# Layer norm by per-token statistics and one activation per token and image; reciprocals read from PSUM

## The chip, the cores and the metric

The kernel runs on one core of a Trainium2 chip. The metric is the device time of one execution in microseconds (us). All data stay in the chip's memory before and after; nothing is computed on the host.

## The reference

The input is x, 16 images of 64 channels by 56x56 pixels, float32. Two layers follow each other.

```
x = x + conv(group_norm(x))                        # grouped correlations, two depthwise convolutions
t = tokens of x: 3136 per image, 64 channels
t = t + attention(layer_norm(t))                   # linear attention, 16 heads of 64, features elu + 1
t = t + experts(layer_norm(t))                     # 32 experts, routing by softmax over tokens
layer_norm(v) = (v - mean(v)) / sqrt(var(v) + 1e-5)      # over the 64 channels of one token
attention: q, k = elu(.) + 1, weighted by cos and sin of the position
           out = (q . sum k v) / (q . sum k + 1e-5)      # the division is by token and head
```

Only the two layer norms and the division of the attention are touched by the change.

## The kernel before

Images are worked on in 8 pairs, the two images side by side, so that a tile of 128 partitions holds 64 channels of both. Seven pairs run in a hardware loop on every engine, and in that loop the convolution of the next pair is computed beside the attention of this one; the eighth pair is a copy of the body without a next pair. A setup stage stands ahead and a final stage (expert matrices, additions, stores) behind. Every engine runs a list of its own in program order and waits on semaphores for the others, so the order written in the functions named pair_of_images is the order of the work.

A pair has these stages.

- **Key stage**, 50 tiles (25 of 128 tokens for each image). TensorE projects a tile (k_project), ScalarE takes the exponential, VectorE makes the feature (k_features), GpSimd weights the tokens by cos and sin, and TensorE multiplies (k_products).
- **Query stage**, 56 slots: 14 steps (7 blocks of 448 pixels for each image) by 4 quarters of the 16 heads. In slot j TensorE projects quarter j (q_project), ScalarE takes its exponential into EQ, and VectorE makes the feature of quarter j-1 (q_features). Later slots deal with quarters that are further along: denominators (den_parts, den_guard, den_reciprocal), reciprocals stored to memory and loaded again, spread over the partitions, into RB by SyncE's queue, the multiplication of a feature by its reciprocal (q_scale, line 1118), the output product (q_output), its weighting (out_parts), the fold and the residual (out_residual). The lags in slots are constants.
- **Drain**, slots 56 to 68, in which the last quarters are finished and the front of the next pair's convolution is computed.
- **Correlations and back**: TensorE's correlations for the next pair, the routing of this pair, the next pair's convolution, and the first layer norm of its first two groups of tokens.

Tokens are normalised in NG = 4 groups of 7, 7, 7 and 4 tiles of 128 tokens, both images at once: 14 or 8 rows of 64 channels on each partition. The first norm (LN1) has groups 0 and 1 in the back stage and groups 2 and 3 in the key stage; the second norm (LN2) has groups 0 and 1 in the query stage and groups 2 and 3 in the drain and after it. norm_part is four parts on VectorE: sums, means and subtraction, squares, sums of squares. deviations, on GpSimd, turns a group's variances into 1/sqrt; norm_scale, on VectorE, multiplies. In LN1 ScalarE's high_part and VectorE's low_part then split the result in two float16 halves for TensorE.

Beside this, in tiles 20 to 49 and slots 3 to 47, 75 taps of the next pair's depthwise convolution are computed: ScalarE multiplies a shifted window by a weight (tap_product, line 723) and GpSimd adds it up (tap_sum, line 591). VectorE has other taps (depthwise, line 936), which lie in the key stage and after the query stage.

PSUM is cut in areas A, B and C of two banks and D and E of one. In the query stage A and B alternate between quarters, E holds denominators and their sums, and outputs alternate between D and C, where C holds the folds too. Each use of an area waits until the one before it was emptied.

## Time and profile before

| | |
|---|---|
| time, median of 3 runs | 3789.2 us (3786.9 to 3798.8) |
| the profiled execution | 3803.7 us, its span 3801.8 us |
| TensorE matmuls busy | 3253.6 us, 86% of the span |
| VectorE busy | 2995.8 us, 79% |
| ScalarE busy | 1746.2 us, 46% |
| GpSimd busy | 1561.9 us, 41% |
| mean granted TensorE clock | 0.942 |

A share of busy time is a mean over stages with different limits. Stages repeat pair by pair, so that one pair of the seven in the loop can be read for all, and the eighth pair shows the same stages without the convolution's work beside them.

### The profile page before, as it was taken

How to read it: one execution, taken by the hardware profiler on the slowest of the kernel's cores; microseconds unless marked ns; L12 is line 12 of the kernel's file. 1: busy time of each engine (PE TensorE's matmuls, PEld its weight loads, DVE VectorE, ACT ScalarE, POOL GpSimd, SP SyncE). 2: the span in 40 equal slices, each digit the busy share in tenths (PEclk: the TensorE clock that was granted, in tenths of full speed). 3: DMA queues.
4: the chain of work that ended last, by engine and by line, in shares of the span. 5: the costliest groups of instructions: out<-in, count | busy, mean ns of one | idle time of the engine just before them, and what ended most of it. 6: DMA issues, size and time to landing. Idle time of an engine off the chain costs nothing.

```text
span 3801.8 us, 50528 instructions
## 1 busy us (share of the span) xinstructions
PE 3253.6 (86%) x16628; PEld 1480.5 (39%) x16628; DVE 2995.8 (79%) x3283; ACT 1746.2 (46%) x1881; POOL 1561.9 (41%) x1078
## 2 busy tenths in 40 slices
PE   4698888988898888988889888898889888898965
PEld 2343334433443335433344334433354333543333
DVE  6887987889687987879878796788877798756843
ACT  1166524754357533665347543465335653343320
POOL 1067611864038631676218650287414762210000
PEclk8899999999999998999999999999999999999977
DMA  2002540044200551025400453005520155204566
GB/s 51 18 1 60 129 105 27 1 109 117 67 27 17 132 128 44 1 60 124 111 27 1 100 117 77 27 1 129 123 51 19 30 129 118 49 1 95 132 155 232
DMA packets 69379, 279.57 MB, mean 74 GB/s; under 512 B 30845, under 2 KB 35485, under 8 KB 64221
## 3 DMA queue, kind: packets, MB, share of 16 engines
q1 hardware_dynamic: 69085, 275.89, 29.8%
q8 instruction: 155, 2.54, 0.3%
q14 instruction: 139, 1.14, 0.1%
HBM read 242.78 MB, written 33.05 MB: 73 GB/s over the span
## 4 chain that ended last, share of the span: by engine, by line
PE 49%; DVE 25%; issue 10%; DMA 8%; ACT 4%; SPq 2%; POOL 1%; DVEq 0%; POOLq 0%; ACTq 0%
PE ps_C L1474 9%; DVE region L1118 5%; PE ps_A L1459 5%; PE ps_B L1459 5%; DMA RB<-r_keep 5%; PE ps_D L1474 4%; DVE region L1110 4%; PE ps_E L1474 4%; PE ps_D L1541 4%; PE ps_C L1541 3%; PE ps_E L1520 3%; DVE arena L936 3%; PE ps_D L1327 3%; PE ps_B L1503 2%; DMA r_keep<-RR 2%
## 5 line engine op out<-in xcount | busy, mean ns | idle before, releaser
L591 POOL TENSOR_TENSOR arena<-arena,UHL 128x896 f32<-128x896 f32 x525 | 1136.9, 2169 | 473.2 <-ACT UHL L723 473.2
L1118 DVE TENSOR_TENSOR region<-region,RB 128x896 f32<-128x896 f32 x448 | 647.0, 1445 | 97.1 <-DMA RB<-r_keep 96.9
L723 ACT ACTIVATE UHL<-arena,W8C 128x896 f32<-128x896 f32 x525 | 542.0, 1032 | 0.0
L569 POOL TENSOR_SCALAR ST<-ST 128x14 f32<-128x14 f32 x64 | 23.7, 371 | 1125.6 <-DVE ST L991 1124.3
L759 ACT ACTIVATE EQ<-ps_B,NEG 128x896 f32<-128x896 f32 x224 | 225.7, 1007 | 545.4 <-PE ps_B L1503 545.4
L1541 PE MATMUL ps_C<-region,small 128*128 128x448 f32 x896 | 409.7, 582 | 24.5 <-DVE region L1118 24.5
L1541 PE MATMUL ps_D<-region,small 128*128 128x448 f32 x896 | 405.7, 577 | 28.0 <-DVE region L1118 28.0
L601 POOL TENSOR_TENSOR UA<-region,CS 128x128 f32<-128x128 f32 (+1 forms) x400 | 229.7, 576 | 419.8 <-PE ps_C L1474 370.7
L1474 PE MATMUL ps_C<-region,UA 128*128 128x512 f32 (+1 forms) x800 | 378.3, 595 | 1.4 <-ACT region L657 1.3
L936 DVE SCALAR_TENSOR_TENSOR arena<-arena,W8C 128x448 f32<-128x448 f32 (+1 forms) x243 | 365.1, 1523 | 0.0
L1520 PE MATMUL ps_E<-region,small 128*32 128x448 f32 x1792 | 231.0, 589 | 155.5 <-DVE region L1110 154.7
L759 ACT ACTIVATE EQ<-ps_A,NEG 128x896 f32<-128x896 f32 x224 | 225.5, 1006 | 267.9 <-PE ps_A L1503 267.9
L1086 DVE SCALAR_TENSOR_TENSOR region<-region,ps_A 128x1024 f32<-128x1024 f32 (+1 forms) x200 | 242.2, 1211 | 106.0 <-ACT region L741 104.2
L1086 DVE SCALAR_TENSOR_TENSOR region<-region,ps_B 128x1024 f32<-128x1024 f32 (+1 forms) x200 | 242.4, 1212 | 105.4 <-ACT region L741 103.6
L741 ACT ACTIVATE region<-ps_A,NEG 128x1024 f32<-128x1024 f32 (+1 forms) x200 | 222.7, 1114 | 199.4 <-PE ps_A L1459 199.4
L741 ACT ACTIVATE region<-ps_B,NEG 128x1024 f32<-128x1024 f32 (+1 forms) x200 | 222.9, 1115 | 168.9 <-PE ps_B L1459 168.8
L1110 DVE SCALAR_TENSOR_TENSOR region<-EQ,ps_B 128x896 f32<-128x896 f32 x224 | 237.4, 1060 | 45.5 <-ACT EQ L759 39.7
L1110 DVE SCALAR_TENSOR_TENSOR region<-EQ,ps_A 128x896 f32<-128x896 f32 x224 | 241.5, 1078 | 26.7 <-ACT EQ L759 23.0
L1541 PEld LDWEIGHTS ps_C<-region,small 128*128 128x128 f32 x896 | 166.3, 199 | 203.9 <-issue 135.1
L1541 PEld LDWEIGHTS ps_D<-region,small 128*128 128x128 f32 x896 | 161.4, 195 | 212.3 <-issue 153.1
L1474 PE MATMUL ps_D<-region,UA 128*128 128x512 f32 (+1 forms) x400 | 205.9, 596 | 0.0
L1474 PE MATMUL ps_E<-region,UA 128*128 128x512 f32 (+1 forms) x400 | 204.2, 592 | 0.0
(296 smaller groups left out, 5063.9 us busy)
## 6 DMA issues: line engine op xcount, KB each, us to landing
RB<-r_keep SPq DMA_DIRECT2D x448, 448.0 KB, 5.8
arena<-x SPq DMA_DIRECT2D x8, 1568.0 KB, 7.2
t_keep<-Y SPq DMA_DIRECT2D x7, 1568.0 KB, 5.2
r_keep<-RR SPq DMA_DIRECT2D x448, 7.0 KB, 1.9
w_keep<-region SPq DMA_DIRECT2D x7, 784.0 KB, 5.9
CST<-t_keep SPq DMA_DIRECT2D x2, 1568.0 KB, 9.2
small<-t_keep SPq DMA_DIRECT2D x2, 1568.0 KB, 12.8
plane<-w_keep SPq DMA_DIRECT2D x4, 784.0 KB, 15.9
```

Of the source, the lines that this page charges most:

```text
L591: pool.tensor_tensor(out=X[:, cut], in0=X[:, cut], in1=PRODUCT[m % 3], op=ALU.add).then_inc(pool_taps.sem, 1)
L723: act.activation(PRODUCT[m % 3].rearrange("p (h w) -> p h w", w=W), g_window(2 * g * ROWS + 2 * (k // 5), 2 * (k % 5) - 4, 2 * ROWS), ACT. ...
L741: act.activation(E[0:r, k % 2], here.area(("kp", k))[0:r, :], ACT.Exp, bias=NEG1[0:r, 0:1]).then_inc(e_ready.sem, 1)
L759: act.activation(EQ[:, j % 2], here.area(key)[:, :] .rearrange("p (c n) -> p c n", c=2)[:, :, 0:PIX], ACT.Exp, bias=NEG1[:, 0:1]).then_inc ...
L936: dve.scalar_tensor_tensor(out=chunk, in0=window, scalar=w[:, k:k + 1], in1=chunk, op0=ALU.mult, op1=ALU.add).then_inc(taps_done.sem, 1)
L1086: dve.scalar_tensor_tensor(out=KT[0:r, k % 3], in0=E[0:r, k % 2], scalar=1.0, in1=here.area(key)[0:r, :], op0=ALU.min, op1=ALU.max)\
L1110: dve.scalar_tensor_tensor(out=Q[s % 3][:, 2 * cc:2 * cc + 2, :], in0=EQ[:, cc % 2], scalar=1.0, in1=here.area(key)[:, :].rearrange("p (c ...
L1118: dve.tensor_tensor(out=q, in0=q, op=ALU.mult, in1=RB[:, cc].rearrange("p (c n) -> p c n", c=2)).then_inc(scaled.sem, 1)
L1459: ins = pe.matmul(here.area(key)[0:r, cut], UTS[i][:, t * P:t * P + r], w[:, cut], start=m == 0, stop=m == 1)
L1474: ins = pe.matmul(dst, UA[0:r, k % 3].rearrange("p s c -> p (s c)"), KT[0:r, k % 3, n * 512:(n + 1) * 512], start=t == 0, stop=t == TILES - 1)
L1520: ins = pe.matmul(here.area(key)[j * STRIP:(j + 1) * STRIP, 0:PIX], KK[i][:, c, :], Q[s % 3][:, c, :], start=g == 0, stop=g == 1)
L1541: ins = pe.matmul(here.area(key)[:, 0:PIX], MW[i][:, c, :], Q[s % 3][:, c, :], start=c == 0, stop=c == NCHUNK - 1)
```

## The change

The layer norms get their statistics from bn_stats and bn_aggr on VectorE, one of each for every tile and image (14 or 8 of each in a group). GpSimd's deviations reads variance and mean from MVL and also makes minus mean times 1/sqrt. The subtraction and the multiplication become one Identity activation on ScalarE for every tile and image (apply_norm), in place, with scale and bias from ST. In the key stage, the query stage and the drain a group's activations are split over two tiles or slots. LN2's slots move, ALL_SLOTS grows by one, and low_part of groups 2 and 3 moves by one tile.

The spread reciprocals are copied by ScalarE from RB to PSUM area C (spread_out, at the lag that q_scale had), the steps from q_scale on come one slot later, and q_scale reads its second operand there. Outputs use D alone, and folds use E. SyncE loads the next half of RB when ScalarE has copied it, not when VectorE has used it. Stage by stage all other work stays where it was.

```diff
--- before.py
+++ after.py
@@ constants
-SPLIT_TILES = [None, 0, 9, 13]
+SPLIT_TILES = [None, 0, 10, 14]
...
-DEN_LAG, SUM_LAG, RECIP_LAG, RB_LAG, OUT_LAG, PARTS_LAG, FOLD_LAG = 4, 5, 5, 9, 10, 14, 19
-FOLD_SLOTS = {8 * n + FOLD_LAG: n for n in range(NPIX)}
+DEN_LAG, SUM_LAG, RECIP_LAG, COPY_LAG, RB_LAG, OUT_LAG, PARTS_LAG = 4, 5, 5, 9, 10, 11, 15
+FOLD_SLOTS = {8 * n + (22 if n < NPIX - 2 else 20): n for n in range(NPIX)}
...
-LN2_SLOTS = {28: 0, 44: 1, 60: 2, 68: 3}
-ALL_SLOTS = 69
+LN2_SLOTS = {31: 0, 47: 1, 61: 2, 69: 3}
+ALL_SLOTS = 70
@@ PSUM areas by use, in pair_uses
-                uses += [(("fold", FOLD_SLOTS[j]), "C")] if j in FOLD_SLOTS else []
+                uses += [(("fold", FOLD_SLOTS[j]), "E")] if j in FOLD_SLOTS else []
...
+                uses += [(("rb", *divmod(j - COPY_LAG, 4)), "C")] if 0 <= j - COPY_LAG < SLOTS else []
...
-                uses += [(("out", (j - OUT_LAG) // 4), "DC"[(j - OUT_LAG) // 4 % 2])] if slot_of_step(j, OUT_LAG) else []
+                uses += [(("out", (j - OUT_LAG) // 4), "D")] if slot_of_step(j, OUT_LAG) else []
@@ SyncE, before it loads half h of RB
-                            sp.wait_ge(*scaled.at(pair, 4 * (s - 1) + 2 * h + 2))
+                            sp.wait_ge(*here.filled(("rb", s - 1, 2 * h + 1)))
@@ GpSimd, deviations
+                st, mv = ST[:, g % 2], MVL[:, g % 2]
                 pool.wait_ge(*sums.at(pair, g + 1))
                 passed(pool)
-                pool.tensor_scalar(ST[:, g % 2, 2, :], ST[:, g % 2, 1, :], 1.0 / C, LN_EPS, ALU.mult, ALU.add)\
-                    .then_inc(variance.sem, 1)
-                pool.wait_ge(*turn)
-                pool.tensor_tensor(out=ST[:, g % 2, 3, :], in0=ST[:, g % 2, 2, :], op=ALU.pow,
-                                   in1=NEGH[:, 0:1].broadcast_to([P, 2 * GROUP])).then_inc(std.sem, 1)
+                pool.tensor_scalar(st[:, 2, :], mv[:, :, 1], LN_EPS, None, ALU.add)
+                pool.tensor_scalar(st[:, 1, :], mv[:, :, 0], -1.0, None, ALU.mult).then_inc(variance.sem, 1)
+                pool.wait_ge(*turn(1))
+                pool.tensor_tensor(out=st[:, 3, :], in0=st[:, 2, :], op=ALU.pow,
+                                   in1=NEGH[:, 0:1].broadcast_to([P, 2 * GROUP])).then_inc(variance.sem, 1)
+                pool.wait_ge(*turn(2))
+                pool.tensor_tensor(out=st[:, 0, :], in0=st[:, 1, :], in1=st[:, 3, :], op=ALU.mult)\
+                    .then_inc(std.sem, 1)
@@ ScalarE, new functions
+            def apply_norm(which, std, ready, pair, g, part=None):
+
+                t, m = GROUPS[g]
+                if part != 1:
+                    act.wait_ge(*std.at(pair, g + 1))
+                wide = C if which == 2 else C - 1
+                for n in range(m if part == 1 else 0, m if part == 0 else 2 * m):
+                    u = UN[which][:, 2 * t + n, 0:wide]
+                    ins = act.activation(u, u, ACT.Identity, bias=ST[:, g % 2, 0, n:n + 1],
+                                         scale=ST[:, g % 2, 3, n:n + 1])
+                if part != 0:
+                    ins.then_inc(ready.sem, 1)
...
+            def spread_out(here, s, cc):
+                key = ("rb", s, cc)
+                act.wait_ge(*spread_loaded[cc // 2].at(here.pair, s + 1))
+                act.wait_ge(*here.room(key))
+                passed(act)
+                act.activation(here.area(key)[:, :].rearrange("p (c n) -> p c n", c=2)[:, :, 0:PIX],
+                               RB[:, cc].rearrange("p (c n) -> p c n", c=2), ACT.Copy)\
+                    .then_inc(*here.fill(key))
@@ ScalarE, where they stand
                 for g in range(2):
+                    apply_norm(1, ln1_std, un1_ready, pair, g)
                     high_part(pair, g)
...
-                    if k in SPLIT_TILES[2:]:
-                        high_part(pair, SPLIT_TILES.index(k))
+                    for part in range(2):
+                        if k - part in SCALE_TILES:
+                            apply_norm(1, ln1_std, un1_ready, pair, SCALE_TILES.index(k - part), part)
+                    if k + 1 in SPLIT_TILES[2:]:
+                        high_part(pair, SPLIT_TILES.index(k + 1))
...
+                    if 0 <= j - COPY_LAG < SLOTS:
+                        spread_out(here, *divmod(j - COPY_LAG, 4))
                     if j in LN2_SLOTS:
                         tokens(here, 2, LN2_SLOTS[j])
+                    for part in range(2):
+                        if j - 7 - part in LN2_SLOTS:
+                            apply_norm(2, ln2_std, un2_ready, pair, LN2_SLOTS[j - 7 - part], part)
...
+                apply_norm(2, ln2_std, un2_ready, pair, NG - 1)
@@ VectorE, norm_part
-                    link(dve.tensor_reduce(out=st[:, 0], in_=u, axis=AX.X, op=ALU.add))
-                    link(dve.tensor_scalar(st[:, 3], st[:, 0], 1.0 / C, None, ALU.mult))
-                elif part == 1:
-                    link(dve.tensor_tensor(out=u, in0=u, in1=st[:, 3].unsqueeze(2).broadcast_to([P, 2 * m, C]),
-                                           op=ALU.subtract))
-                elif part == 2:
-                    link(dve.tensor_tensor(out=SQ[:, 0:2 * m, :], in0=u, in1=u, op=ALU.mult))
+                if part < 2:
+                    for n in range(part * m, (part + 1) * m):
+                        ins = dve.bn_stats(out=BSL[:, g % 2, n, :], in_=UN[which][:, 2 * t + n, :])
+                    if part == 1:
+                        link(ins)
+                        passed(dve)
+                        if which == 1:
+                            dve.memset(UN[1][:, 2 * t:2 * t + 2 * m, C - 1:C], 1.0)
                 else:
-                    dve.tensor_reduce(out=st[:, 1], in_=SQ[:, 0:2 * m, :], axis=AX.X, op=ALU.add)\
-                        .then_inc(sums.sem, 1)
+                    for n in range(2 * m):
+                        ins = dve.bn_aggr(out=MVL[:, g % 2, n, :], in_=BSL[:, g % 2, n:n + 1, :])
+                    ins.then_inc(sums.sem, 1)
...
-            def norm_scale(which, std, pair, g):
...
-                return dve.tensor_tensor(out=u, in0=u, op=ALU.mult,
-                                         in1=st[:, 3].unsqueeze(2).broadcast_to([P, 2 * m, C]))
-
-            def norm1_scale(pair, g):
@@ VectorE, q_scale
-                dve.wait_ge(*spread_loaded[cc // 2].at(here.pair, s + 1))
+                dve.wait_ge(*here.filled(key))
                 dve.tensor_tensor(out=q, in0=q, op=ALU.mult,
-                                  in1=RB[:, cc].rearrange("p (c n) -> p c n", c=2)).then_inc(scaled.sem, 1)
+                                  in1=here.area(key)[:, :].rearrange("p (c n) -> p c n", c=2)[:, :, 0:PIX])\
+                    .then_inc(*here.empty(key))
@@ TensorE, q_output
-                pe.wait_ge(*scaled.at(here.pair, 4 * s + cc + 1))
+                pe.wait_ge(*here.emptied(("rb", s, cc)))
```

The rest of the diff removes the semaphore `scaled` and the tile SQ, adds the tiles BSL and MVL with a memset, and fits the counts of semaphores and the calls of the functions above.

## Rows read from the trace of the kernel before

**Rows 1.** Stages of the fourth pair, and the last pair's query stage; duration, then PE, PEld, DVE, ACT, POOL busy.

```profile
1067.80:1202.00 134.20, 133.22 (x438) 57.78 (x437) 115.71 (x105) 90.38 (x92) 91.16 (x80) 0.99 0.03 12
...
1213.00:1404.70 191.70, 162.63 (x758) 62.73 (x756) 170.38 (x169) 99.33 (x103) 105.51 (x49) 0.96 0.52 118
1404.70:1436.50 31.80, 28.77 (x165) 11.43 (x163) 22.88 (x26) 8.83 (x17) 0.60 (x1) 1.00 0.53 117
1436.50:1512.00 75.50, 59.96 (x558) 39.28 (x558) 52.46 (x71) 25.59 (x30) 14.68 (x11) 0.90 0.13 38
...
3445.60:3620.80 175.20, 157.60 (x758) 62.45 (x756) 145.44 (x174) 57.80 (x58) 5.58 (x4) 0.98 0.58 130
```

**Rows 2.** Sum of the seven query stages of the loop, same columns, then their means.

```profile
sum 1346.40, PE 1140.69 PEld 440.28 DVE 1194.95 ACT 695.54 POOL 738.66; mean PE 162.96 PEld 62.90 DVE 170.71 ACT 99.36 POOL 105.52
```

**Rows 3.** Groups of instructions in the fourth pair's query stage: busy us, mean ns.

```profile
L1118 DVE TENSOR_TENSOR region<-region,RB 128x896 f32<-128x896 f32 x47 | 73.7, 1569 | 4.1 <-DMA RB<-r_keep 4.1
L723 ACT ACTIVATE UHL<-arena,W8C 128x896 f32<-128x896 f32 x45 | 46.5, 1033 | 0.0
...
L1110 DVE SCALAR_TENSOR_TENSOR region<-EQ,ps_B 128x896 f32<-128x896 f32 x27 | 28.6, 1059 | 4.5 <-ACT EQ L759 3.7 <-PE ps_C L1541 0.4 <-DVE SQ L989 0.4
L759 ACT ACTIVATE EQ<-ps_B,NEG 128x896 f32<-128x896 f32 x28 | 28.2, 1007 | 66.6 <-PE ps_B L1503 66.6
...
L1125 DVE TENSOR_TENSOR DS<-ps_E,CST 128x448 f32<-128x448 f32 x13 | 8.0, 617 | 4.4 <-PE ps_E L1520 4.3
...
L1003 DVE TENSOR_TENSOR un<-un,ST 128x896 f32<-128x896 f32 x2 | 3.7, 1842 | 0.0
...
L984 DVE TENSOR_SCALAR ST<-ST 128x14 f32<-128x14 f32 x2 | 3.1, 1540 | 0.1
```

**Rows 4.** The same in the last pair's query stage, where GpSimd adds no taps.

```profile
L1118 DVE TENSOR_TENSOR region<-region,RB 128x896 f32<-128x896 f32 x47 | 51.0, 1084 | 11.7 <-DMA RB<-r_keep 11.7
```

**Rows 5.** Timeline of the fourth pair's query stage: start us, duration us, instruction.

```profile
1212.95 1.01 ACT L759 ACTIVATE EQ<-ps_A,NEG 128x896 f32<-128x896 f32 x1 [5.90 <-PE ps_A L1503]
...
1213.86 1.00 ACT L759 ACTIVATE EQ<-ps_B,NEG 128x896 f32<-128x896 f32 x1
...
1304.77 2.09 POOL L591 TENSOR_TENSOR arena<-arena,UHL 128x896 f32<-128x896 f32 x1 [0.70 <-ACT UHL L723]
...
1305.85 1.96 DVE L1118 TENSOR_TENSOR region<-region,RB 128x896 f32<-128x896 f32 x1
```

**Rows 6.** Groups over the whole span, forms kept apart: small ones, and with a pointer operand or none.

```profile
L655 ACT ACTIVATE un<-ps_B 128x896 f32<-128x896 f32 x24 | 21.8, 910 | 19.7 <-PE ps_B L1378 19.7
...
L779 ACT ACTIVATE region<-ps_B,GBC 64x448 f32<-64x448 f32 x24 | 15.1, 630 | 11.7 <-PE ps_B L1616 11.4
...
L773 ACT ACTIVATE plane<-ps_A 128x448 f32<-128x448 f32 x8 | 4.5, 560 | 5.4 <-PE ps_A L1607 5.4
...
L683 ACT ACTIVATE region<-ps_B 64x64 f32<-64x64 f32 x7 | 1.4, 205 | 0.0
...
L1100 DVE COPY small<-ps_A 64x4 f32<-64x4 f32 x60 | 6.9, 156 | 0.2
...
L884 DVE BATCH_NORM_AGGREGATE MV<-BS 128x2 f32<-128x42 f32 x8 | 2.8, 345 | 1.2 <-DVE BS L880 0.5
```

**Rows 7.** Timeline of the back stage before the fifth pair's first key tile.

```profile
1490.92 1.09 DVE L983 TENSOR_REDUCE ST<-region 128x14 f32<-128x896 f32 x1
...
1495.50 1.08 DVE L983 TENSOR_REDUCE ST<-region 128x14 f32<-128x896 f32 x1
...
1500.08 1.08 DVE L1003 TENSOR_TENSOR region<-region,ST 128x896 f32<-128x896 f32 x1
...
1502.32 1.09 DVE L1015 TENSOR_TENSOR UHL<-region,UHL 128x896 f16<-128x896 f32 x1 [0.83 <-ACT UHL L663]
...
1505.72 0.55 PE L1391 MATMUL ps_E<-IDH,UHL 128*128 128x128 f16 x7 [1.42 <-DVE PT L1046]
...
1510.09 0.60 PE L1459 MATMUL ps_A<-WKH,plane 128*128 128x512 f16 x1 [3.82 <-issue]
```

More of the change, by code:

```diff
@@ L994, in norm_sums @@
             def norm_sums(here, which, sums, g):
-                for part in range(4):
+                for part in range(3):
                     norm_part(here, which, sums, g, part)
-            def norm_scale(which, std, pair, g):
-                t, m = GROUPS[g]
-                u = UN[which][:, 2 * t:2 * t + 2 * m, :]
-                st = ST[:, g % 2, :, 0:2 * m]
-                dve.wait_ge(*std.at(pair, g + 1))
-                return dve.tensor_tensor(out=u, in0=u, op=ALU.mult,
-                                         in1=st[:, 3].unsqueeze(2).broadcast_to([P, 2 * m, C]))
```

40 lines of the change are left out of this document (16 added, 24 removed).

## The prediction

> **What bounds the kernel now.** I read the busy shares first, then a table of stages, then the groups of the query stage, then its timeline. The shares (TensorE 86%, VectorE 79%) name no bound, since stages differ. In the table of stages [rows 1] the key stage is TensorE's: 133.2 us of 134.2 busy, so VectorE's savings there are worth nothing. The query stage is nobody's at first sight: 191.7 us with TensorE at 162.6 and VectorE at 170.4. The last pair does the same query work in 175.2 us, with TensorE at 157.6. What it lacks is GpSimd's taps (POOL 5.6 instead of 105.5) and ScalarE's products for them. VectorE has no taps in either, yet needs 25.0 us less (145.4). So GpSimd's work makes VectorE's slower, and that is the 16.5 us between the two stages. Seven such stages take 1346.4 us, 192.3 each [rows 2].
>
> The groups say where. q_scale takes 1569 ns in the loop's stage [rows 3] and 1084 ns in the last pair's [rows 4]. The timeline shows how: a tap starts on GpSimd at 1304.77 and lasts to 1306.86; q_scale, issued at 1305.85, has two inputs in SBUF and lasts 1.96 us, that is until about 0.95 us after the tap's end [rows 5]. It waits for the tap and only then runs. q_features, which has one input in PSUM, takes 1059 ns beside the same taps, and den_parts 617 ns for half the columns [rows 3]. An input in PSUM keeps an instruction out of this.
>
> **The change: reciprocals from PSUM.** q_scale gets that form, so I price it at 1.065 us. Its bounds are 1.059 (q_features) and 1.084 (its own uncontended time). 47 of them in a query stage save 47 x (1.569 - 1.065) = 23.7 us of VectorE. ScalarE gets 47 copies more. No row has it write to PSUM, so the copy lies between 0.91 us (a read of PSUM, no pointer operand) and 1.03 (tap product) [rows 3, 6]. Consecutive activations overlap: two exponentials of 1.01 us start 0.91 apart [rows 5]. In a slot with a product ScalarE then has about 0.91 + 0.93 + 0.88 = 2.7 us, at most 3.07 without overlap. TensorE's floor for a slot is 175.2 / 56 = 3.13 us. So ScalarE fits, with 0.1 to 0.4 us to spare in each of the 40 or so slots that have all three.
>
> The copies bring new waits. Area C is single, so a copy waits for the q_scale before it, and q_scale for its copy: 1.0 + 1.0 + two semaphores, 2.2 us, under a slot. The exponential behind a copy in ScalarE's order ends some 4.2 us after the slot's start on VectorE, and is due two slots after it, at 6.3: 2 us of slack. Outputs have only D now: q_output's first quarter waits for out_parts, which stands right behind q_features in VectorE's slot. Folds are in E, so the next denominators wait for out_residual, 2.9 us into VectorE's slot. But TensorE is the late one by then. From the second half of a step's denominators on it has two and a half outputs, three projections and the sums, some 8 us of its 12.5 in the step, before it comes to either wait. I price both at nothing. Uncovered, they cost about 1 us in each of 14 steps. For the loads of RB the buffer comes free about a slot's third later than before and is due as much later, so no change.
>
> **The change: layer norms.** On VectorE a full group's sums take 4.58 us now (1490.92 to 1495.50) and the scaling 1.08 [rows 7], and more beside GpSimd: in the query stage the 14-column step takes 1.54 us and the scaling 1.84 [rows 3]. So 5.7 to 7.6 us go for each group. They are replaced by 14 bn_stats and 14 bn_aggr. From 156 ns at 4 columns [rows 6] and 1.08 us at 896 [rows 7] a column costs 1.04 ns, so bn_stats of 64 columns takes 0.22 us and bn_aggr between 0.156 and 0.345 [rows 6]. With about 0.1 overlapped, a group is 14 x (0.12 + 0.15) = 3.8 us; bounds 2.4 (14 x 0.17) and 7.9 (no overlap, 0.345). I take 4.0. Two groups in the query stage give VectorE 7 us more; its load falls to 170.4 - 23.7 - 7 = 140 us, below the last pair's 145.4.
>
> On ScalarE a group is 14 activations with two pointer operands. A 64-column activation without pointers takes 205 ns; one pointer costs 0.07 (630 against 560 ns) to 0.10 (1007 against 910) [rows 3, 6]. So 0.205 + 0.17 = 0.375, started 0.28 to 0.3 apart: 4.0 us a group, bounds 14 x 0.1 = 1.4 and 14 x 0.4 = 5.6.
>
> The Trainium skill (ScalarE: Activation LUTs, What ACT_TABLE_LOAD costs) gives 186 ns + 0.833 ns per element, 93 ns for each pointer operand and 93 ns of overlap, which would be an estimated 0.33 us each and 4.6 us a group. By it the losses below would be a seventh higher.
>
> GpSimd has two small operations more in deviations, about 0.2 and 0.3 us.
>
> **Where the norm's new work lies.** Query stage: group 0 falls into two slots that also have products, 2 us of activations in each, against 2 us of slack and 0.4 regained per slot. I take 2 us lost. Group 1 comes after the products and is covered. Key stage: two tiles in a row get 2 us each on ScalarE beside exponential and high_part, 3.3 and 4.1 us against 2.68 for a tile; 0.8 us lost. Drain: half of group 2 now stands in front of the tokens of group 3, from which the correlations start; 1.0 us. Back: group 0's chain was sums, power, scaling, high_part, low_part at 1502.32, transposes at 1505.72, next key stage at 1510.09 [rows 7]. Now 4 us on ScalarE stand where 1.08 us on VectorE stood, less 0.6 from the sums, plus 0.5 on GpSimd; low_part comes 2.4 to 3 us later. But before, the transposes waited 1.4 us for the routing's copies behind a second scaling that is gone. So they come about 1.1 us later, and ScalarE, with group 1 behind them, makes the first exponential some 0.5 later still: 1.5 us.
>
> **The sum.** The query stage goes from 192.3 to 175.2, the last pair's floor, plus 2 for group 0 and 2 for the tighter coupling of three engines: 179.3, a gain of 13.0. Taken off are 0.8 + 1.0 + 1.5 = 3.3, which leaves 9.7 a pair, 68 us in seven. The last pair and the setup have no GpSimd taps to escape from and pay 6: their last groups lie open. Net -62 us. The profiled execution, 3803.7 us, would come to 3742; it stood 14.5 above the median, and from the median I get 3727.
>
> **Rivals.**
> - *The floor is reached and the norms hide.* The query stage comes to 175 or a little less, since TensorE still waits in the last pair, and the small activations cost half: 17 x 7 - 1 x 7 - 2 = 110 us, 3679. For it: VectorE's load falls under the last pair's. Against: ScalarE goes from 99 to 154 us of the stage. Chance 0.13.
> - *ScalarE's order becomes the bound of the query stage.* A slot then takes what exponential, product and copy need with their waits, 3.3 to 3.4 us where all three stand: 40 x 3.35 + 16 x 3.13 = 184, a gain of 8, and with 4 more for group 0 and 3.3 elsewhere it is next to nothing: -35 to +10, 3754 to 3799, middle 3780. For it: 3.07 us without overlap. Against: the overlap seen in consecutive exponentials. Chance 0.15.
> - *Slower: the small activations lie open.* A pair has 100 of them, 6 x 14 + 2 x 8. At 0.28 to 0.4 us that is 28 to 40 us of ScalarE, in front of exponentials in its order. If 20 us of it reach the path, 13.0 - 20 = -7, and 7 pairs with the 6 us of the ends make it 55 us slower: 3844. It decides from 13 us exposed on, against my 5.3 in all. For it: in the key stage TensorE has 1 us of slack. Chance 0.12.
>
> The Trainium skill (VectorE: DVE Perf Modes, The TRN2 errata) has a rule on that side: operations from SBUF on both engines pay a fixed time for each instruction, and tiles of 512 elements or more should be used. No row here has 64-column activations from SBUF with two pointers; if the rule holds for them, the time is that of this rival or between it and the forecast.
>
> **Chances and range.** The forecast, a query stage shorter by 9 to 16 us and a kernel shorter by 25 to 90, has 0.60. Measurements of this kernel can tell 0.3%, 11 us, from no change. Faster by more than that: 0.60 + 0.13 + a third of the second rival = 0.78. Within it: 0.09, from the second rival. Slower: 0.13, the third and the last of the second. The likeliest case alone would be 3700 to 3760. The range, 3675 to 3785, takes in the floor at the low end and most of the second rival at the high one, and leaves out the slower case.
>
> **What the profile after would show.** q_scale near 1.07 us in all stages, with or without GpSimd; the loop's query stage at 177 to 182 us, ScalarE at about 154 of them; the copy near 0.9 to 1.0 us; the small activations near 0.37 us and 0.28 apart; the key stage longer by about 1 us, and the first key tile 1 to 2 us later behind the sums of LN1. The prediction falls if exponentials come late in many slots, that is if VectorE's idle time behind them (3.7 us a stage for area B now [rows 3]) doubles, or if TensorE waits for VectorE at the first quarter of outputs or at denominators after a fold.

## The result, and the profile after

The changed kernel takes 3733.4 us (median of 4 runs, 3729.7 to 3743.7), the kernel before 3790.7 on the same chip (4 runs, 3786.9 to 3798.8). The ratio is 0.985, with a 95% interval of 0.9825 to 0.9876: 57 us less, where 62 were forecast.

The two profiled executions differ by more, 3803.7 against 3729.7 us. The one of before stood 14.5 us above its median of then, the one of after 3.7 below its own. Stage by stage below, 74 us are therefore shared out, and some 17 of them are the spread of single runs.

Shares and groups over the whole span of the kernel after, for [rows 3, 6]:

```profile
PE 3202.3 (86%) x16628; PEld 1465.8 (39%) x16628; DVE 2668.4 (72%) x4499; ACT 2375.5 (64%) x3129; POOL 1550.8 (42%) x1207
L1144 DVE TENSOR_TENSOR region<-region,ps_C 128x896 f32<-128x896 f32 x448 | 485.5, 1084 | 121.6 <-ACT ps_C L755 117.7
L755 ACT ACTIVATE ps_C<-RB 128x896 f32<-128x896 f32 x448 | 409.4, 914 | 167.7 <-DVE region L1144 99.2
```

q_scale is at 1084 ns over all stages and the copy at 914. VectorE fell from 79% to 72% of the span. Now the windows of one pair's key, query, drain and back stages and of the last pair's query stage, and the sum and mean of the seven query stages (columns as in [rows 1, 2]). The pair is the one that [rows 1] call the fourth. Counted from the first key exponential of the trace it is the third, and is called so from here on:

```profile
1056.00:1191.00 135.00, 132.67 (x433) 56.82 (x432) 111.65 (x137) 97.29 (x114) 92.22 (x84) 0.99 0.00 1
1201.90:1375.60 173.70, 153.96 (x754) 59.71 (x752) 139.55 (x212) 143.39 (x171) 100.38 (x53) 1.00 0.60 131
1375.60:1414.10 38.50, 32.09 (x169) 13.09 (x167) 24.36 (x52) 19.85 (x35) 3.49 (x3) 0.96 0.42 93
1414.10:1492.20 78.10, 59.78 (x567) 39.77 (x566) 41.85 (x122) 42.09 (x81) 14.08 (x17) 0.93 0.16 53
...
3374.80:3542.30 167.50, 154.84 (x754) 60.70 (x752) 140.43 (x217) 104.26 (x126) 6.68 (x8) 0.99 0.61 136
...
sum 1215.90, PE 1080.22 PEld 418.74 DVE 977.10 ACT 1003.78 POOL 702.73; mean PE 154.32 PEld 59.82 DVE 139.59 ACT 143.40 POOL 100.39
```

The query stage went from 192.3 us [rows 2] to 1215.9 / 7 = 173.7. VectorE's load in it fell from 170.7 to 139.6, ScalarE's rose to 143.4, and TensorE's fell too, from 163 to 154.3. Its matmuls are the same but for the four of one fold, some 1 us, which now lie in the drain (754 records for 758): the rest is the granted clock, 1.00 where it was 0.96. The last pair's query stage, 175.2 before, is 167.5. So what the prediction called a floor was none.

The stages of all kernels, from here on, as means over the seven loop pairs. Key is from the first to the last key exponential; 10.9 us follow in every kernel, then query, from its first to its last exponential; drain reaches to the last output product, back to the next pair's first key exponential. The slots of query and drain were shifted against each other by the change, so their sum is what compares. The last column is the time against that of before measured beside it on the same chip, with its 95% interval. The medians come from several chips, on which before took 3790.6 to 3795.7 us.

| kernel | key | query | drain | q. + d. | back | median us | ratio |
|---|---|---|---|---|---|---|---|
| before | 135.6 | 192.3 | 31.9 | 224.2 | 75.7 | 3790.7 | 1 |
| after | 136.2 | 173.7 | 37.6 | 211.3 | 78.1 | 3733.4 | 0.985 |
| reciprocals_only | 135.7 | 177.6 | 38.1 | 215.7 | 73.4 | 3715.8 | 0.9788 (0.9765 to 0.9811) |
| norms_only | 137.0 | 178.8 | 31.5 | 210.3 | 80.7 | 3742.6 | 0.9858 (0.9833 to 0.9883) |
| sbuf_read | 136.3 | 188.4 | 39.8 | 228.1 | 82.1 | 3879.3 | 1.0226 (1.0207 to 1.0246) |
| one_activation | 135.4 | 172.7 | 37.2 | 209.9 | 70.2 | 3646.4 | 0.9612 (0.9592 to 0.9631) |
| less_norm | 134.6 | 181.7 | 30.1 | 211.8 | 75.8 | 3707.3 | 0.9781 (0.9752 to 0.981) |
| half_output | 136.9 | 177.3 | 38.8 | 216.1 | 79.2 | 3772.7 | 0.9946 (0.9927 to 0.9965) |
| copy_twice | 136.9 | 195.3 | 43.2 | 238.5 | 77.9 | 3938.7 | 1.038 (1.0359 to 1.0402) |
| tokens_first | 136.6 | 172.2 | 35.0 | 207.2 | 77.7 | 3704.8 | 0.9766 (0.9746 to 0.9786) |
| vector_tokens | 135.4 | 172.0 | 35.0 | 207.0 | 73.3 | 3666.1 | 0.9678 (0.9657 to 0.9698) |
| vector_wide | 134.8 | 172.3 | 35.0 | 207.3 | 72.1 | 3644.6 | 0.9611 (0.9595 to 0.9627) |
| reciprocals_tokens | 135.2 | 175.3 | 35.2 | 210.5 | 74.1 | 3694.9 | 0.9752 (0.9731 to 0.9773) |
| vector_all | 134.6 | 173.4 | 35.7 | 209.1 | 71.2 | 3661.3 | 0.9647 (0.9627 to 0.9668) |

### The profile page after: what moved, and what is told of

Same layout as the page of the kernel before. It is cut to its first block, busy times and chain, and to the rows that moved or that the text cites. A ratio compares the mean times of both kernels' runs of the same rounds, so it can differ in the third digit from the quotient of the medians.

```text
span 3727.9 us, 54224 instructions
## 1 busy us (share of the span) xinstructions
PE 3202.3 (86%) x16628; PEld 1465.8 (39%) x16628; DVE 2668.4 (72%) x4499; ACT 2375.5 (64%) x3129; POOL 1550.8 (42%) x1207
## 4 chain that ended last, share of the span: by engine, by line
PE 44%; DVE 15%; ACT 15%; issue 11%; DMA 11%; SPq 3%; POOL 1%; ACTq 0%; DVEq 0%; POOLq 0%
PE ps_C L1496 8%; DMA RB<-r_keep 6%; PE ps_D L1563 5%; PE ps_A L1481 5%; PE ps_D L1496 5%; PE ps_E L1496 5%; PE ps_B L1481 4%; DMA r_keep<-RR 4%; ACT region L677 3%; PE ps_D L1349 3%; DVE arena L977 2%; PE ps_E L1542 2%; ACT ps_C L755 2%; ACT EQ L794 2%; DVE region L1144 2%
## 5 line engine op out<-in xcount | busy, mean ns | idle before, releaser
L600 POOL TENSOR_TENSOR arena<-arena,UHL 128x896 f32<-128x896 f32 x525 | 1092.5, 2085 | 425.5 <-ACT UHL L746 425.5
L1563 PE MATMUL ps_D<-region,small 128*128 128x448 f32 x1792 | 779.0, 560 | 71.6 <-DVE OS L1171 40.8
L1144 DVE TENSOR_TENSOR region<-region,ps_C 128x896 f32<-128x896 f32 x448 | 485.5, 1084 | 121.6 <-ACT ps_C L755 117.7
L755 ACT ACTIVATE ps_C<-RB 128x896 f32<-128x896 f32 x448 | 409.4, 914 | 167.7 <-DVE region L1144 99.2
L1563 PEld LDWEIGHTS ps_D<-region,small 128*128 128x128 f32 x1792 | 313.4, 190 | 427.7 <-issue 324.8
L572 POOL TENSOR_SCALAR ST<-MVL 128x14 f32<-128x14 f32 x64 | 26.7, 416 | 1055.8 <-DVE MVL L1032 1053.3
L773 ACT ACTIVATE region<-ps_B,NEG 128x1024 f32<-128x1024 f32 (+1 forms) x200 | 222.4, 1112 | 136.3 <-PE ps_B L1481 136.3
L1542 PE MATMUL ps_E<-region,small 128*32 128x448 f32 x1792 | 216.7, 555 | 63.6 <-DVE region L1135 61.8
L1135 DVE SCALAR_TENSOR_TENSOR region<-EQ,ps_A 128x896 f32<-128x896 f32 x224 | 241.4, 1078 | 37.2 <-ACT EQ L794 36.5
L1525 PE MATMUL ps_A<-plane,WQH 128*128 128x448 f16 x448 | 158.5, 354 | 56.1 <-DVE region L1135 22.4
L1496 PEld LDWEIGHTS ps_C<-region,UA 128*128 128x128 f32 (+1 forms) x800 | 153.1, 193 | 132.4 <-issue 106.2
```

The lines of the kernel that those rows point to most:

```text
L600: pool.tensor_tensor(out=X[:, cut], in0=X[:, cut], in1=PRODUCT[m % 3], op=ALU.add).then_inc(pool_taps.sem, 1)
L755: act.activation(here.area(key)[:, :].rearrange("p (c n) -> p c n", c=2)[:, :, 0:PIX], RB[:, cc].rearrange("p (c n) -> p c n", c=2), ACT.C ...
L773: act.activation(E[0:r, k % 2], here.area(("kp", k))[0:r, :], ACT.Exp, bias=NEG1[0:r, 0:1]).then_inc(e_ready.sem, 1)
L1135: dve.scalar_tensor_tensor(out=Q[s % 3][:, 2 * cc:2 * cc + 2, :], in0=EQ[:, cc % 2], scalar=1.0, in1=here.area(key)[:, :].rearrange("p (c ...
L1144: dve.tensor_tensor(out=q, in0=q, op=ALU.mult, in1=here.area(key)[:, :].rearrange("p (c n) -> p c n", c=2)[:, :, 0:PIX])\
L1496: ins = pe.matmul(dst, UA[0:r, k % 3].rearrange("p s c -> p (s c)"), KT[0:r, k % 3, n * 512:(n + 1) * 512], start=t == 0, stop=t == TILES - 1)
```

## The experiments

### Each half alone

reciprocals_only has the copies to PSUM with the layer norms of before; norms_only has the new layer norms with q_scale reading RB. Each is the one half of the diff above, with the lags and slots of its half; LN2's new slots went with the copies.

> The kernel before with the reciprocals' half of the change alone (copy to PSUM, lags, areas, LN2's slots); the layer norms stay on VectorE as before. My theory: the gain is q_scale's freedom from GpSimd, so q_scale is 1.08 us in all stages, query stage and drain together fall from 224 us to 212 to 215, key stage and back stage stay at 135.6 and 75.7, and the time is 3700 to 3725 us, a little under the changed kernel's 3733. Rival, the norms bring the gain: 3765 or more.

> The changed kernel without the reciprocals' half; q_scale reads RB in SBUF, with the old lags and areas. My theory: q_scale stays near 1.55 us in the loop's query stages, VectorE's lighter norms give some 2 us there, key and back stage lose 3 us together, and the time is 3780 to 3805 us, no gain. Rival, the norms bring the gain: 3760 or less.

Measured: 78 us less with the copies alone, and 51 less with the norms alone, where my theory gave the norms no gain. Together they bring 57: less than the copies alone. So the first expectation's theory held, but so did the second's rival, that the norms bring a gain. In norms_only q_scale still takes 1400 ns on average over all stages (1445 before) and 1512 in the third pair's query stage (1569), so most of its gain is not q_scale's. Query stages of the third pair, reciprocals_only and then norms_only:

```profile
1197.30:1375.10 177.80, 157.09 (x753) 60.26 (x752) 146.70 (x168) 136.70 (x150) 100.10 (x49) 0.98 0.56 129
```

```profile
1214.80:1393.20 178.40, 157.50 (x758) 61.90 (x756) 158.06 (x213) 108.25 (x131) 109.47 (x53) 0.97 0.55 126
```

The norms took 12.6 us off VectorE in the stage (170.7 to 158.1) and the stage lost 13.5; the copies took off 24.0 and the stage lost 14.7. From either one the other half takes only 4 to 5 us more: VectorE goes from 158.1 to 139.6 us and the stage from 178.8 to 173.7, about a quarter of the relief; after the copies it goes from 146.7 to 139.6 for 3.9 us, about half. So the norms' relief was worth its full size where it came first, the larger one of the copies some 60%, and each about half of that as the second.

With the drain, which the copies lengthen, the halves look different: query and drain are 13.9 us shorter with the norms alone, 8.5 with the copies alone, and 12.9 with both. On top of the norms the copies gain nothing there, as they stand in this change; what they add a pair is 2.6 us in the back stage (80.7 to 78.1) and 0.8 in the key stage, and the runs don't show why. (One query stage of norms_only, the first pair's, took 185.9 us; the other six have 177.6 in the mean.)

### A relief of VectorE and nothing else

less_norm is the kernel before; the layer norm over the outputs (LN2) leaves out the subtraction and the squares.

```diff
+                elif which == 2 and part < 3:
+                    return
```

> The kernel before without the subtraction and the squares of LN2 (parts 1 and 2; this leaves out part of the second norm). VectorE has 2.2 us less a group, 4.3 us in a query stage, and nothing else changes. Theory A, up to some 12 us the query stage follows VectorE's busy time one for one: query stage 192.3 - 4.5 = 188 us, last pair 175.2 - 4.3 = 171, and the time falls by 30 to 45 us. Theory B, the norms shortened the stage in another way (their moved slots, fewer waits of VectorE on itself): less than 2 us a stage, under 15 us in all.

Measured: 3707.3 us, 86 less, nearly twice the most that I expected. This is its third pair's query stage and the last pair's:

```profile
1191.60:1373.70 182.10, 158.72 (x758) 61.91 (x756) 163.36 (x165) 99.36 (x103) 108.73 (x49) 0.97 0.53 124
...
3352.00:3518.40 166.40, 154.03 (x758) 61.66 (x756) 140.78 (x171) 57.82 (x58) 5.58 (x4) 1.00 0.61 136
```

For 7.0 us less on VectorE the stages of the loop lost 10.6; the last pair's lost 8.8 (175.2 to 166.4) for 4.7 us less. ScalarE and GpSimd had nothing new. 4.6 of the 7.0 us are the parts left out; 2.1 are q_scale, which met fewer taps (1524 ns in the third pair's stage, 1569 before). TensorE's busy time fell as well, from 162.6 to 158.7 us for the same 758 matmuls. What the relief sets free is seen in the kernel before, in windows of 6 us around LN2's group in the third pair, and in instructions of VectorE there:

```profile
1308.00:1314.00 6.00, 2.56 (x8) 0.85 (x8) 5.60 (x5) 3.18 (x4) 2.93 (x2) 1.00 0.63 153
1314.00:1320.00 6.00, 5.31 (x24) 1.99 (x24) 5.77 (x6) 0.17 (x1) 3.24 (x3) 0.72 0.42 104
...
1326.00:1332.00 6.00, 3.23 (x16) 1.10 (x13) 6.00 (x5) 3.74 (x4) 3.68 (x3) 1.00 0.62 153
1332.00:1338.00 6.00, 6.00 (x26) 2.39 (x27) 5.26 (x6) 0.93 (x2) 1.33 (x1) 0.72 0.42 93
```

```profile
1302.55 1.54 DVE L984 TENSOR_SCALAR ST<-ST 128x14 f32<-128x14 f32 x1
...
1310.03 2.32 DVE L1118 TENSOR_TENSOR region<-region,RB 128x896 f32<-128x896 f32 x1
...
1328.31 2.60 DVE L1003 TENSOR_TENSOR un<-un,ST 128x896 f32<-128x896 f32 x1
```

VectorE is full there (5.6 and 6.0 of 6 us), with operations of the norm and q_scales stretched by the taps. TensorE has little to do (2.56 and 3.23 of 6 us), and in the next 6 us the granted clock is at 0.72, part of the time at its 1.2 GHz level, just when TensorE has the backlog to work off. The stall is paid twice. That less_norm, with nothing else changed, raised the clock of the last pair's stage from 0.98 to 1.00 and cut both stages by more than VectorE was relieved of is the evidence for this. The 48 us around this group, before and then after:

```profile
1290.00:1338.00 48.00, 38.83 (x174) 15.11 (x174) 45.25 (x42) 21.65 (x24) 26.18 (x13) 0.93 0.47 109
```

```profile
1291.00:1339.00 48.00, 42.40 (x203) 16.37 (x202) 38.58 (x71) 42.48 (x57) 32.39 (x18) 1.00 0.61 134
```

After the change, the clock is at 1.00 throughout, and 203 matmuls are done where 174 were.

### Is TensorE the floor now?

half_output is the kernel after with one of two matmuls of each q_output left out; half of the heads are missing from the outputs. copy_twice is the kernel after with one more activation of the copy's size ahead of each copy.

```diff
-                for c in (2 * cc, 2 * cc + 1):
+                for c in (2 * cc,):
```

```diff
+                act.activation(SPARE[:, :], RB[:, cc], ACT.Copy)
```

> The changed kernel with one of the two matmuls of each q_output left out, so half of the heads are missing in the output; TensorE has 0.8 us less in each slot, 45 us less in a query stage. Theory A, TensorE is the floor of the query stage after the change (154 us busy of 174): the stage falls by 8 us or more, to VectorE's order, and the time by 100 us with the drains. Theory B, the loop of the three engines through single areas is the floor: the stage falls by less than 4 us.

> The changed kernel with a second activation of RB into a spare tile in front of each copy to PSUM, 0.93 us more of ScalarE in each of 56 slots, standing between q_scale and the copy that the next q_scale waits for. Theory A, ScalarE has 0.3 to 0.4 us to spare in slots with taps: the query stage grows by 20 to 30 us, ScalarE being its bound. Theory B, ScalarE has the slack that its busy time shows (30 us of 174): under 10 us.

```profile
1214.40:1388.10 173.70, 130.95 (x664) 44.19 (x662) 138.68 (x212) 142.44 (x171) 100.38 (x53) 0.94 0.58 130
```

```profile
1254.40:1449.30 194.90, 160.59 (x754) 60.34 (x752) 139.75 (x212) 180.04 (x217) 100.34 (x53) 0.97 0.51 116
```

half_output: 3772.7 us, 39 more than the kernel after, which neither theory had. With 90 matmuls and 23 us less of work TensorE is idle for 42.7 us of this stage, and the stage is not shorter; the one shown is the shortest of seven, whose mean is 177.3. In its drain the clock is at 0.85. So TensorE's amount of work did not bound the stage, and with less work on it the granted clock was lower, not higher. The two are not told apart here: the stage might be shorter with half of the work at the old clock. copy_twice: the query stage grew by 21.6 us, as theory A had it. 46 of the 56 added activations lie in the stage and make ScalarE busy for 36.6 us more, of which 15 found room in its idle time; it is busy for 180.0 of 194.9 us now, and is the bound there. That it is close to the bound in the kernel after (143.4 of 173.7), but not alone, is argued.

### Who reads what: sbuf_read

This one keeps the copies, and lets q_scale read RB in SBUF all the same; SyncE waits for q_scale as before.

```diff
-                                  in1=here.area(key)[:, :].rearrange("p (c n) -> p c n", c=2)[:, :, 0:PIX])\
+                                  in1=RB[:, cc].rearrange("p (c n) -> p c n", c=2))\
```

> The changed kernel with one operand changed back: the copy to PSUM is still made and waited for, but q_scale reads RB in SBUF, and SyncE loads RB again only when q_scale has used it. My theory (two SBUF inputs wait for GpSimd's additions): q_scale at 1.5 to 1.9 us beside taps and 1.08 in the last pair, the loop's query stage at 190 us or more, time 3790 to 3840 us. Rival, the new lags and the lighter norms made the query stage short: q_scale longer or not, the time stays within 15 us of 3733.

Measured: 3879.3 us, 2.3% slower than before and 146 us slower than after. The query stage is 188.4 us, 14.7 longer than after, a little less than I expected. The time is more than I expected: drain and back stage are 2.2 and 4.0 us longer than after. That copy and q_scale take turns, so that each late q_scale makes the next copy and the next load late, would lengthen the drain; what lengthens the back stage is not shown. Its timeline, GpSimd and then VectorE:

```profile
1302.09 2.08 POOL L600 TENSOR_TENSOR arena<-arena,UHL 128x896 f32<-128x896 f32 x1 [1.40 <-ACT UHL L746]
```

```profile
1303.10 2.03 DVE L1144 TENSOR_TENSOR region<-region,RB 128x896 f32<-128x896 f32 x1
...
1307.73 1.09 DVE L1144 TENSOR_TENSOR region<-region,RB 128x896 f32<-128x896 f32 x1 [0.50 <-ACT ps_C L755]
```

The tap ends at 1304.17, and q_scale, issued at 1303.10, ends 0.96 later, as in [rows 5]; the one at 1307.73 meets no tap and takes 1.09. With two inputs in SBUF q_scale is at 1463 ns in the mean over all stages, 1587 to 1623 in the loop's query stages and 1089 in the last pair's, and up to 2872; with one in PSUM it is at 1083 to 1086 in every kernel. The Trainium skill (SBUF — State Buffer, SBUF: two separate sides) describes an exclusive lock on a port pair that VectorE and GpSimd share: of a VectorE instruction with two inputs in SBUF and a GpSimd instruction that reads SBUF, the first to start holds it for its whole length and the other waits; the trace agrees, by the 0.96 us after the tap's end.

### The price of the small activations

one_activation is the kernel after with one activation of the whole part (x 0.5) in place of its 7 or 14; the normalisation is left out.

```diff
-                for n in range(m if part == 1 else 0, m if part == 0 else 2 * m):
-                    u = UN[which][:, 2 * t + n, 0:wide]
-                    ins = act.activation(u, u, ACT.Identity, bias=ST[:, g % 2, 0, n:n + 1],
-                                         scale=ST[:, g % 2, 3, n:n + 1])
+                low, high = m if part == 1 else 0, m if part == 0 else 2 * m
+                u = UN[which][:, 2 * t + low:2 * t + high, 0:wide]
+                ins = act.activation(u, u, ACT.Copy, scale=0.5)
```

> The changed kernel with the 14 (or 8) small activations of a group replaced by one wide Copy with factor 0.5 for each part; this leaves the normalisation itself out. ScalarE saves about 3.5 us a group, 26 us a pair. My theory: some 2 us in the query stage, 0.8 in the key stage, 1 in the drain and 2.5 to 3 in the back stage were exposed, so the time falls by 40 to 55 us to 3680 to 3695. Rival, small activations are hidden: within 12 us of 3733. Rival, they lie open in large part: under 3650.

Measured: 3646.4 us. Against after it is 87 us less by medians, 77 by the profiled executions. That is twice what I expected, and just in the range of the rival that they lie open in large part. A pair is 10.1 shorter: 7.9 of them in the back stage, where I had 2.5 to 3, 1.4 in query and drain, where I had 3, and 0.8 in the key stage. So the back stage has nearly all of it. The timeline of the kernel after in the back stage ahead of the fourth pair, for [rows 7]:

```profile
1466.79 1.87 DVE L1024 BATCH_NORM_STATS2 BSL<-region 128x6 f32<-128x64 f32 x14
...
1469.79 1.83 DVE L1024 BATCH_NORM_STATS2 BSL<-region 128x6 f32<-128x64 f32 x14
...
1473.67 2.42 ACT L677 ACTIVATE region<-region,ST 128x63 f32<-128x63 f32 x7 [2.88 <-POOL ST L578]
1478.44 0.95 ACT L685 ACTIVATE UHL<-region 128x896 f16<-128x896 f32 x1
...
1482.86 4.72 ACT L677 ACTIVATE region<-region,ST 128x63 f32<-128x63 f32 x14
1484.87 0.60 PE L1481 MATMUL ps_A<-WKH,plane 128*128 128x512 f16 x1 [3.15 <-issue]
1487.61 0.95 ACT L685 ACTIVATE UHL<-region 128x896 f16<-128x896 f32 x1
1492.17 1.11 ACT L773 ACTIVATE region<-ps_A,NEG 128x1024 f32<-128x1024 f32 x1 [3.61 <-issue]
```

The sums of a group take 3.0 us from one group to the next. Group 0's chain lets TensorE make the first key tile at 1484.87. But ScalarE then has group 1: 14 activations for 4.72 us, high_part until 1488.56, and 3.61 us on its way round the loop. The first key exponential starts at 1492.17, 7.3 us after TensorE began the key tiles; before it was 1.9 (1510.09 to 1512.01). From the first sum to it are 25.4 us, before 21.1 (1490.92 to 1512.01). TensorE itself is not late: from the first sum to the first key tile are 18.1 us, before 19.2.

### Mending it: tokens_first, vector_tokens, vector_wide, reciprocals_tokens, vector_all

The drain of the kernel after, from its timeline:

```profile
1393.93 0.92 ACT L755 ACTIVATE ps_C<-RB 128x896 f32<-128x896 f32 x1 [2.74 <-DMA RB<-r_keep]
1394.88 0.92 ACT L664 ACTIVATE un<-ps_A 128x896 f32<-128x896 f32 x1
1395.94 4.19 PE L1327 MATMUL ps_A<-arena,W2T 64*64 64x448 f32 x24 [2.96 <-ACT un L664]
...
1402.42 1.15 DVE L977 SCALAR_TENSOR_TENSOR arena<-arena,W7C 128x896 f32<-128x896 f32 x1 [5.55 <-ACT arena L654]
```

ScalarE stands before a copy whose load has not landed; tokens (L664), which wait for nothing more, stand behind it, TensorE waits 2.96 us for the area that they empty, and VectorE 5.55 for what comes of it. tokens_first exchanges the two in the slot:

```diff
-                    if 0 <= j - COPY_LAG < SLOTS:
-                        spread_out(here, *divmod(j - COPY_LAG, 4))
                     if j in LN2_SLOTS:
                         tokens(here, 2, LN2_SLOTS[j])
+                    if 0 <= j - COPY_LAG < SLOTS:
+                        spread_out(here, *divmod(j - COPY_LAG, 4))
```

> The changed kernel with tokens in front of spread_out in ScalarE's slot. Theory A, the drain is 6 us longer than before because a copy that waits for RB's load holds up the tokens of group 2, and TensorE's front waits for their area: drain 37.6 down by 3 us or more, time down by 15 to 30 us. Theory B, the drain is longer because of its one slot more and of copy and q_scale taking turns: within 8 us of 3733.

Measured: 3704.8 us, 29 less than after, of which 2.6 us a pair in the drain, a little under the 3 expected, and 1.5 in the query stage.

vector_tokens adds to tokens_first that VectorE applies LN1's groups 0 and 1 in the back stage, by two wide instructions with operands of ST broadcast; vector_wide adds LN1's groups 2 and 3 and LN2's 2 and 3, so that the small activations stay in the query stage alone. vector_all moves those two groups as well. reciprocals_tokens is reciprocals_only with the exchange.

```diff
-                    apply_norm(1, ln1_std, un1_ready, pair, g)
...
+                link(dve.tensor_tensor(out=u, in0=u, op=ALU.mult,
+                                       in1=st[:, 3].unsqueeze(2).broadcast_to([P, 2 * m, wide])))
+                dve.tensor_tensor(out=u, in0=u, op=ALU.add,
+                                  in1=st[:, 0].unsqueeze(2).broadcast_to([P, 2 * m, wide]))\
+                    .then_inc(ready.sem, 1)
```

> tokens_first, and groups 0 and 1 of LN1 in the back stage scaled on VectorE by two wide operations (multiply, add; 2.2 us a group) in place of 14 small activations (4.7 us). Theory A, the small activations of the back stage stand on its path: back stage 77.7 down by 3 to 6 us, time 3670 to 3685 against tokens_first's 3705. Theory B, they are covered there and the 8 us that one_activation saved in the back stage came from the others: within 8 us of 3705.

> vector_tokens, and also LN1's groups 2 and 3 in the key stage and LN2's groups 2 and 3 behind the query stage scaled on VectorE by two wide operations; small activations stay in the query stage alone. Theory A, the small activations in the drain and behind it hold up ScalarE's columns for the correlations: 1 to 4 us less a pair, 3645 to 3675. Theory B, with VectorE's order in place of ScalarE's the gain is given back: at or above vector_tokens.

> The reciprocals' half alone (norms as in the kernel before) with tokens in front of spread_out. Theory A, the wait that tokens_first removed comes from the copies and not from the norms: 3716 falls by 15 to 30 us to 3686 to 3701. Theory B, it needs the small activations: within 8 us of 3716.

> vector_wide with LN2's groups 0 and 1 in the query stage scaled on VectorE too, so that no small activation is left. These two wide operations have both inputs in SBUF, so beside taps they wait for GpSimd. Theory A, the query stage is VectorE's and ScalarE's nearly alike (139.7 and 143.5 us busy) and VectorE's waits cost more than their length: query stage up by 3 to 8 us from 172, time 3665 to 3700, slower than vector_wide's 3645. Theory B, small activations cost there what they cost elsewhere: the stage falls by 1 to 4 us, time 3620 to 3640.

Measured: 3666.1, 3644.6, 3694.9 and 3661.3 us. In vector_tokens the back stage lost 4.4 us, as theory A had it, and the time came 4 us under its range; vector_wide came out at the low end of its own. In reciprocals_tokens the exchange is worth 21 us without any small activation, so the wait that it removes comes with the copies. vector_wide is the best of all kernels here: 3.9% under before, 89 us under after. Its back stage, and the chain in it:

```profile
1384.40:1456.20 71.80, 57.41 (x558) 38.28 (x558) 49.74 (x130) 25.38 (x31) 13.38 (x17) 0.93 0.13 39
```

```profile
1442.04 1.08 DVE L1040 TENSOR_TENSOR region<-region,ST 128x882 f32<-128x882 f32 x1 [0.83 <-POOL ST L578]
...
1451.66 0.94 ACT L685 ACTIVATE UHL<-region 128x896 f16<-128x896 f32 x1
...
1456.18 1.11 ACT L772 ACTIVATE region<-ps_A,NEG 128x1024 f32<-128x1024 f32 x1 [3.57 <-PE ps_A L1498]
```

The first key exponential now waits for TensorE's scores and not for ScalarE's own queue. vector_all shows where the small activations do pay: with LN2's groups 0 and 1 on VectorE too, the query stage and the drain are 1.8 us longer, the back stage is 0.9 shorter and the kernel 17 us slower by medians (14 by the ratios). Its way is theory A's, but the query stage grew by 1.1 us and not by 3 to 8, and the two profiled executions are only 6 us apart. So the sign of this step is shown and its size is not.

## Why the prediction was right, point by point

The time, 3733, is 6 us from the 3727 forecast, and the sum is close for each stage of a pair:

| term | forecast | measured |
|---|---|---|
| query and drain | -13.0 + 1.0 = -12.0 | -18.6 + 5.7 = -12.9 |
| key | +0.8 | +0.6 |
| back | +1.5 | +2.3 |
| a pair | -9.7 | -9.9 |
| setup, last pair, tail | +6 | -5 |

So the total is near by luck in part: a query stage 5.6 us better than forecast is set off by a drain 4.7 worse (a part of each is the boundary between them, which moved by a slot), and the sum over the two profiled executions is 74 us where the medians differ by 57. (The prediction's 175.2 + 2 + 2 is 179.2, a gain of 13.1, not 179.3 and 13.0; it changes nothing.)

**"So GpSimd's work makes VectorE's slower, and that is the 16.5 us between the two stages": half right.** q_scale went to 1084 ns (1065 taken) and sbuf_read shows that its operand in PSUM does it. But norms_only reached nearly the same stage as reciprocals_only (178.8 to 177.6) with q_scale still at 1512 ns in it, and less_norm 181.7. What counts is VectorE's load where it bunches, that is where norm and stretched q_scales fill several slots in a row, whoever makes it.

**"The last pair's floor", 175.2 us: the step that failed.** The prediction let the stage fall to 175.2 and no further, as "TensorE's floor for a slot". That stage fell to 167.5 itself, and to 166.4 by less_norm alone; in half_output it was 167.0 with 25 us less of TensorE's work. In the last pair of before VectorE still held TensorE up, and the clock with it. TensorE is busy for 8.6 us less in the loop's stage (163.0 to 154.3), 1 of them the fold that moved and the rest the clock (0.96 to 1.00). The sum had no term for it. The 4 us put on top for group 0 and the coupling, and the drain's 5.7 in place of 1.0, hid this in the total. So did the ends: I put 6 us on them since they "have no GpSimd taps to escape from", and the last pair's query and drain are 4.8 us shorter.

**The drain, +1.0 taken: mis-sized, for another reason.** With the boundary moved by a slot its own part can't be read off; but tokens_first took 2.6 us of it away by the order alone. "For the loads of RB the buffer comes free about a slot's third later than before and is due as much later, so no change": the copy waits for them in ScalarE's order, and what stands behind it was not named. The store of r_keep (the reciprocals) also lands in 4.0 us where it took 1.9. It does so in all kernels with the copies (3.9 to 4.9) and in none without (1.9); why, no run shows.

**The back stage, +1.5 taken: near in the stage, wrong in both terms.** The stage is 2.3 us longer. From its first sum on, as means over the seven pairs, the first key tile comes 0.8 us earlier (18.4 for 19.1) where the prediction had it 1.1 later, since low_part moved by 1.2 us (third pair) and not 2.4 to 3. The exponential comes 4.1 us later (25.2 for 21.0). So the term "ScalarE, with group 1 behind them, makes the first exponential some 0.5 later still" had the place and was mis-sized: it measures 4.9 us (from 1.9 to 6.8 behind the first key tile). The work ahead of the first sum is 1.8 us shorter (54.7 to 52.9), which no term had and which hides the rest. one_activation gives the whole exposure of the small activations as 7.9 us a pair.

**The prices.**

| | taken | measured |
|---|---|---|
| copy to PSUM | 0.91 to 1.03 us | 0.914 |
| q_scale | 1.065 | 1.084 |
| sums of a group on VectorE | 4.0 | 3.0 |
| bn_stats, bn_aggr, each | 0.22, 0.156 to 0.345 | 0.209, 0.151 |
| small activation | 0.375, 0.28 to 0.3 apart | 0.428, 0.33 apart |
| a group of 14 | 4.0 | 4.7 |
| ScalarE in the query stage | 154 | 143.4 |

```profile
L677 ACT ACTIVATE un<-un,ST 128x64 f32<-128x64 f32 x21 | 7.3, 428 | 0.0
L1024 DVE BATCH_NORM_STATS2 BSL<-un 128x6 f32<-128x64 f32 x28 | 3.8, 206 | 0.0
L1032 DVE BATCH_NORM_AGGREGATE MVL<-BSL 128x2 f32<-128x6 f32 x28 | 2.1, 151 | 0.0
```

These are rows of the query stage after. The Trainium skill (ScalarE: Activation LUTs, What ACT_TABLE_LOAD costs) gave an estimate of 0.33 us each and 4.6 a group, and it was nearer than my sum from rows.

**Waits priced at nothing.** TensorE waits for out_parts 4.4 us in the query stage (row below), now that outputs have area D alone. q_scale waits for its copy 13.0 us, 20 times in 46, of the 34 us in which VectorE is idle there. The longest such wait is 2.3 us: the turns fit under a slot, as forecast, but they are not free. Two signs by which the prediction said that it would fall thus came in part: TensorE waits at outputs, and VectorE's idle time behind the exponentials of area B went from 3.7 to 6.6 us. The gain came all the same, so they were no test of it. Waits of the third pair's query stage after (sum, count, longest), and the row of area B's features:

```profile
DVE region L1144 <- ACT ps_C L755: 13.0, 20, 2.3
...
PE ps_D L1563 <- DVE OS L1171: 4.4, 4, 1.7
...
L1135 DVE SCALAR_TENSOR_TENSOR region<-EQ,ps_B 128x896 f32<-128x896 f32 x27 | 28.7, 1062 | 7.2 <-ACT EQ L794 6.6 <-DVE BSL L1024 0.6
```

**The rivals.** "The floor is reached and the norms hide" had the right query stage and the wrong rest: small activations don't cost half, they cost 10 us a pair, by one_activation. "ScalarE's order becomes the bound" gave 184 us, where 173.7 were measured; copy_twice finds some 15 us of room on ScalarE. "The small activations lie open" by 20 us fell, but 10.1 a pair are open against my 5.3. The Trainium skill's rule against small tiles from SBUF (VectorE: DVE Perf Modes, The TRN2 errata) has its direction right: one_activation, with wide tiles on the same engine, is 87 us under the kernel after. Which engine takes the wide tiles is a question of its own: vector_wide is 60 us under tokens_first, while in the query stage VectorE is the dearer engine (vector_all, +17 us).

**What stays open.** Why the query stage stops at 172 to 174 us in all kernels with both halves. TensorE is busy for 154 us of it, ScalarE for 143 and VectorE for 140; half_output speaks against the first alone, though with a lower clock, and copy_twice gives the second 15 us of slack. That three engines which hand areas to each other in turns would stop there is only argued. A second area for the copies wasn't tried: areas A to E fill PSUM.

## What to carry to other kernels

Before a stage that has less of something (here the last pair, without taps) is taken for a floor, see whether the same waits stand in it: a relief of 7 us on the engine whose work bunches brought 10.6 here, and two reliefs of the same bunch don't add up. Add a stage up with the one behind it before you call it shorter. Put many small instructions on the engine with slack in the stage, and nowhere on the chain around a loop's end, where an engine's last work before the branch delays its first work behind it. In an in-order queue, an instruction that waits for a transfer goes behind those that another engine waits for: exchanging two lines was worth 29 us, half of what the change brought.

## What the runs showed of the hardware

- A stall of TensorE cost twice here, the second time by its clock. In the kernel before, two windows of 6 us with TensorE busy for 2.56 and 3.23 us were followed by windows with a granted clock of 0.72. The mean clock over the profiled execution went from 0.942 to 0.957 by the change and to 0.969 in vector_wide. With half of the output matmuls gone it is 0.924, 0.94 in the query stage, and the kernel is 39 us slower.
- bn_stats of 64 columns starts every 0.13 us (14 in 1.87), bn_aggr every 0.07: sums by these two cost 3.0 us for 896 columns, where two reductions, the mean, the subtraction and the squares took 4.58 [rows 7].
- At the loop's end ScalarE is idle for 3.61 us and TensorE for 3.15 before their first work of the next pair, with nothing that they wait for in the trace. Ahead of the eighth pair, which is no pass of the loop, ScalarE goes from high_part to the first key exponential without a pause in the same kernel:

```profile
3234.90 0.95 ACT L685 ACTIVATE UHL<-region 128x896 f16<-128x896 f32 x1
3235.75 1.10 ACT L773 ACTIVATE region<-ps_A,NEG 128x1024 f32<-128x1024 f32 x1
```
